# Two edits on VectorE in a fused attention and FFN kernel: an int32 cast folded into the scaling that reads it, and a state update written as two instructions

## What is computed

```python
def reference(x, Wk, bk, Wv, bv, Wq, bq, Wo, bo, w_gate, w_up, w_down):   # x: 32 x 2048 x 1024
    x = x + layernorm(attn(layernorm(x)))
    x = x + layernorm(ffn(layernorm(x)))
# attn: k, v, q = x Wk^T, x Wv^T, x Wq^T (+ biases), width 128
#   out_t = state q_t;  state = 0.99 state + 0.01 v_t k_t^T   (a recurrence over 2048 positions)
#   y = out Wo^T + bo
# ffn: h = silu(x wg^T) * (x wu^T), width 3072;  y = h wd^T  (int weights times 1/127)
# layernorm(x) = (x - mean) / sqrt(var + 1e-5)
```

## Time and profile before

| what | value |
|---|---|
| median of 3 runs | 2700.57 us (2700.26 to 2812.35) |
| the profiled execution | 2698.0 us |
| its span on the slowest core (core 2) | 2696.5 us (eight cores: 2685.7 to 2696.5) |
| PE busy | 2332.5 us (87% of the span) |
| DVE busy | 1578.0 us (59%) |
| ACT busy | 606.9 us (23%) |
| mean granted TensorE clock, core 2 | 0.986 |

### The profile page before, as it was taken

One profiled execution on the slowest core, in us unless ns is written; L12 is line 12 of the kernel. 1 busy time (PEld: TensorE's weight loads), 2 busy tenths in 40 slices (PEclk: granted clock), 3 DMA queues, 4 the chain that ended last, 5 costly groups with the idle time before them and its releaser, 6 DMA issues.

```text
span 2696.5 us, 52561 instructions; the slowest of 8 cores (2685.7 to 2696.5 us)
## 1 busy us (share of the span) xinstructions
PE 2332.5 (87%) x17504; PEld 1660.3 (62%) x17792; DVE 1578.0 (59%) x5346; ACT 606.9 (23%) x1633; POOL 62.4 (2%) x85
## 2 busy tenths in 40 slices
PE   2879888889889889889898889898888898888897
PEld 1546666666666666666666666666666666666665
DVE  4535565565665565665565665655665655655653
ACT  1222122222122222122222222221222221222211
POOL 4410000000000000000000000000000000000000
PEclk7989999999999999999999999999999999999999
DMA  9950111000000000000000000000000000000000
GB/s 152 140 70 18 32 33 32 32 1 32 33 32 32 32 1 32 32 32 32 32 2 32 32 32 32 21 13 32 32 32 32 11 23 32 33 32 32 1 17 32
DMA packets 76410, 90.56 MB, mean 34 GB/s; under 512 B 56432, under 2 KB 56560, under 8 KB 76144
## 3 DMA queue, kind: packets, MB, share of 16 engines
q1 hardware_dynamic: 19008, 67.12, 7.1%
q0 software_dynamic: 57136, 20.06, 7.0%
HBM read 73.67 MB, written 33.55 MB: 40 GB/s over the span
## 4 chain that ended last, share of the span: by engine, by line
PE 49%; DVE 21%; issue 9%; DVEq 8%; DMA 6%; ACT 5%; ACTq 2%; POOL 0%; POOLq 0%
PE pb L546 15%; PE pb L535 14%; PE pb L525 14%; DVEq L654 7%; DVE X L427 3%; PE pb L334 3%; DVE hT L555 3%; DMA wu_sb<-wub 3%; ACT x1T L258 2%; ACTq L654 2%; ACT x1T L262 2%; DVE X L422 2%; DVE tt L235 2%; DVE tt L236 2%; DVE tt L234 2%
## 5 line engine op out<-in xcount | busy, mean ns | idle before, releaser
L546 PE MATMUL pb<-x3T,wu_sb 128*128 128x256 bf16 x6144 | 800.5, 273 | 86.7 <-DVE hT L555 73.3
L535 PE MATMUL pb<-x3T,wg_sb 128*128 128x256 bf16 x6144 | 801.3, 274 | 58.0 <-DVE x3T L513 34.9
L535 PEld LDWEIGHTS pb<-x3T,wg_sb 128*128 128x128 bf16 x6144 | 588.2, 98 | 266.8 <-issue 98.1
L525 PE MATMUL pb<-wd_sb,hT 128*128 128x512 bf16 x2785 | 726.0, 381 | 15.9 <-issue 1.1
L546 PEld LDWEIGHTS pb<-x3T,wu_sb 128*128 128x128 bf16 x6144 | 582.8, 98 | 204.2 <-issue 135.8
L540 ACT ACTIVATE hT<-pb 128x256 bf16<-128x256 f32 x768 | 293.0, 382 | 1726.2 <-PE pb L535 1444.5
L555 DVE TENSOR_TENSOR hT<-hT,pb 128x256 bf16<-128x256 bf16 x768 | 321.3, 418 | 512.5 <-PE pb L546 505.4
L525 PEld LDWEIGHTS pb<-wd_sb,hT 128*128 128x128 bf16 x3072 | 300.5, 98 | 209.5 <-issue 12.5
L321 PE MATMUL pb<-identb,xhat 128*128 128x128 bf16 x512 | 39.5, 221 | 74.2 <-DVE xhat L312 48.3
L427 DVE SCALAR_TENSOR_TENSOR X<-pb,rr,X 128x512 f32<-128x512 f32 x128 | 96.1, 751 | 11.5 <-issue 0.9
L235 DVE TENSOR_TENSOR tt<-tt,uu 128x2 f32<-128x2 f32 (+1 forms) x480 | 77.0, 160 | 39.5 <-issue 3.1
(11 more groups left out here) (77 smaller groups left out, 1389.8 us busy)
## 6 DMA issues: line engine op xcount, KB each, us to landing
X<-x SPq DMA_DIRECT2D x64, 512.0 KB, 4.0
out<-X SPq DMA_DIRECT2D x64, 512.0 KB, 2.9
wg_sb<-wgb POOLq DMA_DIRECT2D x24, 256.0 KB, 15.0
wu_sb<-wub POOLq DMA_DIRECT2D x24, 256.0 KB, 15.4
wd_sb<-wdb POOLq DMA_DIRECT2D x24, 256.0 KB, 15.2
wq_sb<-wqT POOLq DMA_DIRECT2D x1, 256.0 KB, 8.2
wk_sb<-wkT POOLq DMA_DIRECT2D x1, 256.0 KB, 18.4
wv_sb<-wvT POOLq DMA_DIRECT2D x1, 256.0 KB, 20.9
```

What stands on the lines that cost most here:

```text
L525: mm(lambda E, j=j, jp=jp, lb=lb, dh=dh, dbk=dbk: E.matmul(bank[dbk][:], hT[:, jp * 256 + lb * 128: jp * 256 + (lb + 1) * 128], wd_sb[:, j ...
L535: mm(lambda E, j=j, dc=dc: E.matmul(bank[2][:, 0:256], wg_sb[:, j * 1024 + dc * 128: j * 1024 + (dc + 1) * 128], x3T[:, dc * 256:(dc + 1) ...
L546: mm(lambda E, j=j, dc=dc: E.matmul(bank[3][:, 0:256], wu_sb[:, j * 1024 + dc * 128: j * 1024 + (dc + 1) * 128], x3T[:, dc * 256:(dc + 1) ...
```

## The change

The first edit takes the cast L229 out of `rsqrt_step_list`: the scaling reads the bits of `u` as int32 directly. The list has 15 steps in place of 16, so AQ has 4 steps fewer per tile and EPI_REST one. The second edit writes the state update as a `tensor_scalar` (scale in place) and a `tensor_tensor` (add the bank), both in the same step as before.

```diff
@@ rsqrt_step_list
                 lambda: P.emit("dve", lambda E: E.tensor_scalar(u[:, cs], vsrc, eps, None, ALU.add), reads=vkeys, writes=(ku,)),
-                lambda: P.emit("dve", lambda E: E.tensor_copy(t_[:, cs], u[:, cs].bitcast(I32)), reads=(ku,), writes=(kt_,)),
-                lambda: P.emit("dve", lambda E: E.tensor_scalar(i_[:, cs], t_[:, cs], -0.5, MAGIC, ALU.mult, ALU.add), reads=(kt_,), writes=(ki,)),
+                lambda: P.emit("dve", lambda E: E.tensor_scalar(i_[:, cs], u[:, cs].bitcast(I32), -0.5, MAGIC, ALU.mult, ALU.add), reads=(ku,), writes=(ki,)),
@@ build_A, stup
-                    P.emit("dve", lambda E: E.scalar_tensor_tensor(
-                        stf[:, gs], stf[:, gs], LAMC, bank[5][:, 128:256], ALU.mult, ALU.add),
-                        reads=(("stf", gb), ("bank", 5)), writes=(("stf", gb),))
+                    P.emit("dve", lambda E: E.tensor_scalar(stf[:, gs], stf[:, gs], LAMC, None, ALU.mult),
+                           reads=(("stf", gb),), writes=(("stf", gb),))
+                    P.emit("dve", lambda E: E.tensor_tensor(stf[:, gs], stf[:, gs], bank[5][:, 128:256], ALU.add),
+                           reads=(("stf", gb), ("bank", 5)), writes=(("stf", gb),))
```

## The result

The changed kernel takes 2813.6 us (median of 10 runs), the kernel before 2700.7 us in the same comparison. The ratio is 1.043 (95% interval 1.041 to 1.046): slower by 4.3%. The forecast was 2788 us with a range of 2725 to 2828. The direction and the range hold; the size was 26 us short. Some executions of most kernels are slowed by a lower clock on one or both dies; the ratios leave those out, and where they shift a median (first edit alone, second edit alone, PE kept busy ahead of q) I go by the ratio.

A forecast was written before the change was run, and what follows sets the result against it. A chain changing hands between PE and DVE was taken as the bound. To the profiled 2698.0 us it added 55 (order), 33 (clock) and -1 (casts): 2785, plus 2.6 for the median, so 2788 us, range 2725 to 2828.

The forecast's parts named there:

- The moved steps, blocks 5 to 9: Blocks 5 to 9: q projection 1.57 us later behind apply4, partly regained; carried as +0.91 us in 30 tiles.
- Blocks 10 to 18: Blocks 10 to 18: up(16) 0.55 us later, up(18) about 0.35 more; net +0.90 us in 31 tiles.
- The order as a whole: Both block ranges, 5 to 9 and 10 to 18, summed over their tiles: 55 us slower.
- The state update: 64 added DVE instructions of 0.2 us plus up to 0.1 drain, costing nothing on the path; uncovered, 19 us.
- The clock: PE falls to 1.2 GHz after longer waits ahead of q and up(16): +33 us, bounds 0 to +77.
- the first kind: PE's 2.8 us wait ahead of the q projection, once per tile; a fall after half: 24 us.
- The second kind: PE's 2.46 us wait ahead of up(16), once per tile; a fall after 0.45 of them: 17 us.
- The casts, by count: 160 DVE casts removed, 0.235 us each; 38 us faster if all lay on the path.
- the clock does not follow: Rival: the order costs time but clock falls stay as rare as before; 2755 us, chance 0.18.
- half is absorbed: Rival: the wait ahead of q is hidden elsewhere, only some 0.9 us per tile stay; 2729 us, chance 0.14.
- faster: Rival: four AQ casts leave the path per tile, moved large steps fall into DVE waits; 29 us gain, 2671, chance 0.07.
- A fall nearly every time: Rival: the clock falls after nearly every long PE wait, ahead of q and up(16); 2832 us, chance 0.11.

The follow-up runs named there:

- PE kept busy ahead of q: Changed kernel plus 16 unused 128x256 matmuls per tile on PE, ahead of the q projection: ratio 1.030, about 2780 us.
- the epilogue's count kept: Changed kernel with an empty step put back only in the rsqrt list of EPI_REST, the AQ lists staying one step shorter: 2715.1 us, ratio 1.005.

## Why the prediction was right, and where it was short

- *"The moved steps, blocks 5 to 9"*, in the tiles of the timelines: q came 965.35 - 943.20 = 22.15 us behind gate(0) of its tile, against 1091.08 - 1070.48 = 20.60 before, **+1.55**, forecast +1.57. From q to gate(8) it is 974.22 - 965.35 = 8.87 us, less 1.67 for the clock 7.20, against 8.44: **-1.24**, forecast -1.25. From gate(8) to gate(9) it is 4.47 us (974.22 to 978.69) against 3.60 (1018.79 to 1022.39 in the trace of before): **+0.87**, forecast +0.70. L381 started 0.87 us after L372 where I had 0.76. The rows not shown so far, first of the changed kernel, then of before:

```profile
943.20 1.03 PE L535 MATMUL pb<-x3T,wg_sb 128*128 128x256 bf16 x8 [1.10 <-DVE x3T L513]
```

```profile
1018.79 1.04 PE L535 MATMUL pb<-x3T,wg_sb 128*128 128x256 bf16 x8
...
1022.39 1.03 PE L535 MATMUL pb<-x3T,wg_sb 128*128 128x256 bf16 x8
...
1070.48 1.03 PE L535 MATMUL pb<-x3T,wg_sb 128*128 128x256 bf16 x8 [1.10 <-DVE x3T L513]
```

- *"Blocks 10 to 18"*: up(16) waits 0.53 us longer (2.46 against 1.93), forecast 0.55. From up(16) to up(18) it is 5.75 us (1004.54 to 1010.29); the forecast start of up(18), 0.35 later than the shift of up(16), and the 0.37 us wait agree. The blocks 12 to 14, which I had at net 0, lost about 0.1: up(13) waits 0.35 us.
- The order as a whole: forecast 55 us, measured 62 to 63. In the means over all tiles without a fall the replay's first terms came out close: q +1.39 us, q to gate(8) -1.23, gate(9) to up(16) +0.45. Two were too small: gate(8) to gate(9) is +0.90 against 0.70, and up(16) to up(18) +0.60 against 0.35. Together +2.11 us per tile against 1.82.
- *"The state update"*: no cost, as forecast. The instruction takes 0.22 us; I had taken 0.2 and up to 0.1 for a drain. The table of costs in the Trainium skill ("VectorE: DVE Perf Modes", The TRN2 errata), with the double rate of its section The perf-mode tier table, gave an estimate near 0.13. The same section says that this row comes out too low for a single operation, and gives about 150 cycles as the fixed term measured on a bf16 copy; with that term the estimate is 0.22, and the trace agrees (219 ns in the median).
- *"The clock"*: the mechanism held, the size did not. I took "a fall after half of the first kind, 15 x 1.6 = 24 us". It was 226 of 240 waits on the eight cores, so 28 per core, at 1.67 us each: 47 us. The second kind was overrated: 67 of 240, or 8 per core, against my 14, and at some 8 us in all against my 17. All falls together cost 55 us where I had 41, and the falls that before had were 3 per core, 4 us, where I took off 8. Net 51 us against 33. So the clock term made 18 of the 26 us by which the forecast was short, and the order 7 or 8. That the direction and the range held is not luck: the waits are where the replay put them. The share of one half was a guess between none and all, and it was far off.
- *"The casts, by count"*: the 24 us that the cast's removal gives with all steps in place are about 64% of the 38 us that its time adds up to. The Trainium skill's advice for chained DVE operations ("VectorE: DVE Perf Modes", Rules for kernel authors), to minimise their count, holds in this kernel only with the placing held still.
- The rivals: the clock did follow (against *the clock does not follow*), little was absorbed (against *half is absorbed*), and *faster* was true of the cast's removal alone, at 2676 us, once the steps stay in place. *A fall nearly every time* came true ahead of q (94%) and not ahead of up(16) (28%). The chances gave 0.05 to more than 54 us faster, though the only rival on that side was worth 29 us.

What stays open: a wait of about 2.46 us ahead of up(16) went with a fall in 28 of 184 cases in the changed kernel, and in 126 of 184 with the epilogue's count kept. For the waits of 2.7 to 2.8 us it was 39 of 56 and 56 of 56. A longer wait falls more often within a kernel, but length alone doesn't set it. I know of the difference only that the falls ahead of q are there in one and not in the other.

## What to carry to other kernels

Where side work is woven into a main stream by counting steps, removing one instruction moves all that follow, and a large step can land ahead of the one instruction that the critical engine waits for. Keep the position with an empty step and measure the edit apart from the shift; then place by the time that each step takes on the engine that is tight. And price a new wait on TensorE twice: for itself, and for the clock behind it.

## What was not expected

- Added matmuls that nobody reads made the kernel faster by some 33 us, and with those ahead of up(16) by 55.
- A wait of 2.8 us once per tile let the clock fall in 94% of the tiles (226 of 240), while the 184 waits of 1.9 us ahead of up(16) in the kernel before never did.
- Removing the wait ahead of q raised the falls at the other place, from 67 to 182, and giving PE work in that wait raised them to 140. So the gain of taking away one cause of falls is less than its count times 1.67 us.
- A placing by rough costs of 0.24 to 0.78 us per instruction gave 109 us, and 131 with the cast gone, where I had expected 60 with the cast gone.
